# Attention and convolution block: normalisation and one addition moved to GpSimd, one copy to ScalarE, slot tables redrawn

## The chip, the cores and the metric

The program runs on one core of one Trainium2 chip. The metric is the device time of one execution in microseconds, median of several runs.

## The reference

Eight images x of 256 channels by 32x32 pixels (L = 1024 positions), all in fp32. Each image goes through two stages that matter here.

```
# stage 1: attention over the pixels, 8 heads of 32 channels
xn  = group_norm(x, 32 groups) * gn_w + gn_b
q, k, v = w_qkv @ xn + b_qkv                 # per head 32 x 1024 each
h   = w_proj @ (softmax(q'k / sqrt(32)) v) + b_proj
x   = x + h
# stage 2: tokens t = x transposed (1024 x 256)
n1  = layernorm(t)                           # norm 1
q,k = elu(n1 @ Wqk + bqk) + 1                # linear attention, rotary turn
a   = turn(q) (turn(k)^T n1 / n) * z         # z = 1 / (q . mean k + 1e-6)
t   = t + a + conv3(n1) + lepe_b             # depthwise convolution, width 3
n2  = layernorm(t)                           # norm 2
t   = t + n2 with its 2x2 Haar low band replaced by fc2(gelu(fc1(interp(low band))))
out = t transposed
```

## The kernel before

Stage 1 of image i and stage 2 of image i-1 run in one body, so there is a prologue, a first body (stage 1 of image 0 alone), six steady bodies, a last body and an epilogue (stage 2 of image 7), here called the tail. A body has 64 attention units, one for each of 2 head groups x 8 key blocks x 4 heads. In a unit, TensorE makes a 128x1024 block of scores in one of two PSUM buffers ps_s (L653), VectorE takes the negative maximum (L1053), ScalarE the exponential with its sum (L914). After every four units VectorE inverts the sums (`invert`, L1059), GpSimd scales the values with them (`scale`, L1330) and TensorE weighs the values (`values`, L668). The scores of unit s+2 wait for the exponential of unit s.

All other work is cut in steps and hung between the units by hand-written tables: one for each engine and kind of body, name -> slot numbers. Each engine runs, in each slot s, its unit instruction and then the steps due at s, in the order in which the table names them (`due`). GpSimd has no unit instruction: for it the slots give an order and nothing else. SP issues DMAs in the order of SP_ORDER. All queues are in order; semaphores join them. Results of TensorE for the steps go to two PSUM banks `work` in turn (in the tail six, four of them in ps_s); a tile may be written once the reader of the tile before it in that bank is done (READ, `claim`).

The steps that matter here, for image i-1, with the line where each works:

- proj (L727, VectorE L1153): projection, added to the residual x1, which a DMA has loaded (`residual`); x1T (L707): transposed to tokens, copied to tok by ScalarE (L965).
- stats of norm 1 (L1118, L1123), rsqrt1 on GpSimd (L1361, L1364), norm1 on VectorE (L1129): tok becomes (tok - mean) x r. lnT (L715, L977): transposed back to channels, ln_ch.
- qk (L741, ScalarE L988 and L991, VectorE L1236 `elu`), kT (L749, VectorE L1181 and L1183: turned keys), kv (L757, L1163), den and denT (L768, L774, L1189, L1191), turn on GpSimd (L507 to L514: turned queries), out (L781, VectorE L1199 into t2).
- lepe on GpSimd (L1386, L1389): the convolution, added to x1 in channels. uT (L707): that sum transposed to tokens; VectorE adds it to t2 from PSUM (L1205). Then statistics of norm 2, rsqrt2 on GpSimd, norm2 on VectorE (L1129, t2 to tok), add on GpSimd (L520, t2 + tok), pairs on GpSimd (L1395: sums of neighbours, csum).
- ll (L795, copied L996): the low band; fc1 (L800, gelu L999), fc2 (L805, L1212), rT (L715, L1003): t2 back to channels; spread: four DMAs lay the new band out for late_up (L1224), which adds it to the image; late_store writes it.
- warm: pairs of 128x128 matmuls without a use for their result (L867), in the first body and in the tail.
- For image i+1: load, group statistics (stats, moments, gn, squares, affine, apply), pq, pk, pv: queries, keys and values (L680, L692; hi L955, lo L1098).

## Time and profile before

| | us |
|---|---|
| median of 3 runs (lowest 1364.17, highest 1369.44) | 1364.28 |
| the profiled execution | 1364.11 |
| its span, first to last instruction | 1362.3 |
| TensorE / VectorE / ScalarE / GpSimd busy | 1235.3 / 995.1 / 879.5 / 467.4 |
| mean granted TensorE clock, share of full | 0.976 |

PE is TensorE's matmuls, PEld its weight loads, DVE VectorE, ACT ScalarE, POOL GpSimd, SPq SyncE's DMA queue. Lnnn is a line of the kernel. "Idle before" is the time an engine stood before an instruction, and what is behind the arrow ended that wait. Matmuls overlap, so the busy share of PE is an upper reading.

### The profile page before, as it was taken

The numbers are of one execution on the slowest core, as the hardware profiler recorded it, in microseconds if no ns is written. First come the engines' busy times: TensorE is split into PE (matmuls) and PEld (weight loads), VectorE is DVE, ScalarE is ACT, GpSimd is POOL, SyncE is SP. The second block draws the span as 40 slices with busy tenths as digits, with TensorE's granted clock in tenths as the row PEclk, the third lists the DMA queues.
The fourth block names the chain that finished last, engine by engine and source line by source line (L and its number), as shares of the span: only waits on it lengthen the run. The fifth ranks groups of instructions, "written<-read, shape, count | busy, mean of one in ns | idle before, by whom it ended". The sixth has DMA issues, their size and how long they took to land.

```text
span 1362.3 us, 22187 instructions
## 1 busy us (share of the span) xinstructions
PE 1235.3 (91%) x7972; PEld 644.5 (47%) x7972; DVE 995.1 (73%) x1609; ACT 879.5 (65%) x1457; POOL 467.4 (34%) x621
## 2 busy tenths in 40 slices
PE   6888899899998999899998999989998999979796
PEld 5544444544445454445444444454544444444373
DVE  3666687857889487866888578884879678884663
ACT  1666667675776668676775767766685767757422
POOL 2001017520285015630185203840166301850351
PEclk9998999999999999999999999999999999999897
DMA  8242415123442236223351234422262234300210
GB/s 275 58 108 45 106 40 134 34 63 101 110 112 47 52 109 139 48 63 93 92 116 27 66 117 101 105 57 58 88 140 48 62 93 110 80 15 0 80 33 31
DMA packets 51180, 110.84 MB, mean 81 GB/s; under 512 B 15456, under 2 KB 15840, under 8 KB 50816
## 3 DMA queue, kind: packets, MB, share of 16 engines
q1 hardware_dynamic: 48400, 100.39, 30.3%
q0 software_dynamic: 2480, 8.78, 2.3%
q8 instruction: 64, 1.05, 0.3%
q14 instruction: 44, 0.36, 0.1%
q10 hardware_dynamic: 192, 0.26, 0.1%
HBM read 21.81 MB, written 8.39 MB: 22 GB/s over the span
## 4 chain that ended last, share of the span: by engine, by line
PE 54%; DVE 29%; ACT 7%; issue 4%; POOL 2%; DMA 2%; SPq 1%; DVEq 0%; ACTq 0%; POOLq 0%
DVE negmax L1053 15%; PE ps_s L653 13%; PE ps_o L668 7%; PE work L741 6%; ACT probs L914 5%; PE work L680 4%; PE work L800 4%; PE work L727 4%; PE work L692 3%; DVE tok L1129 3%; DVE ln_st L1118 3%; PE work L805 3%; PE work L781 2%; DVE lo L1098 1%; PE work L715 1%
## 5 line engine op out<-in xcount | busy, mean ns | idle before, releaser
L914 ACT ACTIVATE probs<-ps_s,negmax 128x1024 f32<-128x1024 f32 x512 | 571.0, 1115 | 328.0 <-DVE negmax L1053 323.3
L1053 DVE TENSOR_REDUCE negmax<-ps_s 128x1 f32<-128x1024 f32 x512 | 618.8, 1216 | 220.0 <-PE ps_s L653 218.2
L653 PE MATMUL ps_s<-q_st,k_st 128*128 128x512 f32 x1024 | 407.8, 482 | 54.7 <-ACT probs L914 42.7
L653 PEld LDWEIGHTS ps_s<-q_st,k_st 128*128 128x128 f32 x1024 | 165.1, 192 | 294.4 <-ACT probs L914 163.3
L1330 POOL TENSOR_TENSOR v_scaled<-v_tok,rsums 128x128 f32<-128x128 f32 x128 | 56.0, 438 | 580.3 <-DVE rsums L1059 580.3
L668 PE MATMUL ps_o<-probs,v_scaled 128*32 128x512 f32 x2048 | 249.9, 606 | 1.3 <-POOL v_scaled L1330 1.3
L680 PE MATMUL work<-xg,w_qkv 128*128 128x512 f32 x256 | 120.7, 597 | 2.7 <-ACT xg L927 2.7
L741 PE MATMUL work<-ln_ch,w_qk 128*128 128x512 f32 x240 | 115.0, 601 | 3.6 <-DVE k_ch L1236 3.6
L668 PEld LDWEIGHTS ps_o<-probs,v_scaled 128*32 128x32 f32 x2048 | 53.9, 110 | 129.9 <-issue 117.7
L1389 POOL TENSOR_TENSOR x<-x,csum 128x1024 f32<-128x1024 f32 x45 | 107.5, 2389 | 2.5
L914 ACT ACTIVATION_READ_ACCUMULATOR probs<-ps_s,negmax 128x1 f32 x512 | 99.6, 195 | 0.0
L1361 POOL TENSOR_TENSOR ln_var<-ln_mv,con 128x2 f32<-128x2 f32 x64 | 12.9, 202 | 184.4 <-DVE ln_mv L1123 184.4
L800 PE MATMUL work<-band,w 128*128 128x512 f32 x120 | 63.6, 666 | 7.8 <-ACT band L996 6.0
L680 PEld LDWEIGHTS work<-xg,w_qkv 128*128 128x128 f32 x256 | 46.6, 189 | 44.2 <-issue 38.3
L692 PEld LDWEIGHTS work<-w_qkv,xg 128*128 128x128 f32 x512 | 63.6, 196 | 4.1 <-DVE lo L1098 1.4
L692 PE MATMUL work<-w_qkv,xg 128*128 128x128 f32 x512 | 64.0, 280 | 0.0
L741 PEld LDWEIGHTS work<-ln_ch,w_qk 128*128 128x128 f32 x240 | 43.0, 188 | 42.7 <-issue 29.8
L727 PE MATMUL work<-att,w_proj 128*128 128x512 f32 x120 | 56.8, 597 | 0.0
L1386 POOL TENSOR_SCALAR csum<-ln_ch,par 128x1024 f32<-128x1024 f32 x45 | 54.9, 1221 | 0.0
L805 PE MATMUL work<-shared,w 128*128 128x512 f32 x112 | 52.6, 592 | 0.0
L999 ACT ACTIVATE shared<-work,par 128x512 f32<-128x512 f32 x60 | 41.0, 689 | 16.2 <-PE work L800 16.1
L988 ACT ACTIVATE t<-work,par_elu 128x512 f32<-128x512 f32 x60 | 41.2, 687 | 10.9 <-PE work L741 10.9
(157 smaller groups left out, 1448.5 us busy)
## 6 DMA issues: line engine op xcount, KB each, us to landing
q_st<-hi SPq DMA_DIRECT2D x128, 128.0 KB, 2.4
q_st<-lo SPq DMA_DIRECT2D x120, 128.0 KB, 2.4
...
k_st<-hi SPq DMA_DIRECT2D x128, 64.0 KB, 2.8
k_st<-lo SPq DMA_DIRECT2D x128, 64.0 KB, 3.2
...
```

What stands on the lines that cost most here:

```text
L653: mm = pe.matmul(ps_s[s % 2][:, half * HALF:half * HALF + HALF], k_st[:, h, j * P:j * P + P], q_st[g][:, h, half * HALF:half * HALF + HALF ...
L668: mm = pe.matmul(ps_o[D * h:D * h + D, cols], v_scaled[:, j % 2, D * h:D * h + D], probs[:, j % 2, h, cols], start=(j == 0), stop=(j == NB ...
L680: mm = pe.matmul(bank(tile)[:, :], w_qkv[:, c, col:col + P], xg[:, c, half * HALF:half * HALF + HALF], start=(c == 0), stop=(c == NC - 1))
L692: mm = pe.matmul(bank(tile)[:, P * n:P * n + P], xg[:, c, P * nb:P * nb + P], w_qkv[:, c, col:col + P], start=(c == 0), stop=(c == NC - 1))
L727: mm = pe.matmul(ps[:, :], w_proj[:, g, P * c:P * c + P], att[:, g, half * HALF:half * HALF + HALF], start=(g == 0), stop=(g == 1))
L741: mm = pe.matmul(ps[:, :], w_qk[:, c, col:col + P], ln_ch[:, c, 1 + half * HALF:1 + half * HALF + HALF], start=(c == 0), stop=(c == NC - 1))
L800: pe.matmul(ps[:, :], w1[:, P * n:P * n + P], band[:, :], start=True, stop=True)\
L805: mm = pe.matmul(ps[:, :], w2[:, k, :], hid[:, k, :], start=(k == 0), stop=(k == 7))
L914: act.activation(probs[:, j % 2, h, :], ps_s[s % 2][:, :], ACT.Exp, bias=negmax[:, s % 4:s % 4 + 1], accum_out=sums[:, j % 2, h:h + 1]).th ...
L1053: dve.tensor_reduce(negmax[:, s % 4:s % 4 + 1], ps_s[s % 2][:, :], AX_X, ALU.max, negate=True)\
L1330: pool.tensor_tensor(v_scaled[:, j % 2, :].rearrange("p (h d) -> p h d", h=HG), v_tok[g][:, j, :].rearrange("p (h d) -> p h d", h=HG), r.t ...
L1389: pool.tensor_tensor(x1[:, c, :], x1[:, c, :], lepe_product, ALU.add).then_inc(lepe_step, 1)
```

## The change

1. Except for the last image, the layer norms (norm1, norm2) leave VectorE. GpSimd makes the shift -mean x r (two 128x1 instructions), waits for it, and writes x times r plus shift (two 128x256).
2. Except for the last image, uT is copied from PSUM to tok by ScalarE (signal u_copied, which also frees the bank), and GpSimd adds tok to t2 (`usum`).
3. proj, qk, pq, pk and values are split in two steps for TensorE, the second run right behind the first when both have the same slot; the second part of proj and qk waits for its own input only.
4. In the last image queries come before keys, and the second group's keys, turned keys and the turned queries get buffers of their own in probs, so that waits between the groups fall away.
5. All slot tables and SP_ORDER are redrawn.

```diff
 PE_STEADY = {
-    "proj": (4, 5, 7, 8), "denT": (32,), "lnT": (15, 15, 16, 17), "kv": (28, 32), "out": (35, 36, 40, 41), "ll": (48,),
-    "uT": (38, 39, 42, 42), "rT": (47, 50, 50, 51), "fc2": (52, 54, 56, 57), "pq1": (11, 12), "x1T": (9, 9, 10, 13),
+    "proj": (4, 5, 7, 8), "denT": (32,), "lnT": (15, 15, 16, 17), "kv": (28, 33), "out": (35, 36, 40, 41), "ll": (48,),
+    "uT": (37, 38, 42, 43), "rT": (47, 47, 50, 50), "fc2": (52, 55, 56, 57), "pq1": (11, 13), "x1T": (9, 9, 10, 13),
...
 ACT_STEADY = {
-    "pq0": (43, 44), "x1T": (9, 9, 11, 14), "rT": (47, 50, 50, 51), "copy": (3, 5, 34, 35),
+    "uT": (37, 38, 42, 43), "pq0": (43, 46), "x1T": (9, 10, 11, 14), "rT": (47, 47, 50, 50), "copy": (3, 5, 34, 36),
...
 DVE_STEADY = {
-    "norm1": (11, 14, 16, 16), "norm2": (42, 45, 46, 47), "uT": (39, 40, 42, 43), "late_up": (0, 5),
-    "invert": (2, 5, 8, 12, 16, 20, 25, 28, 32, 36, 41, 44, 48, 54, 56, 60), "moments": (38,), "out": (37, 37, 41, 41),
+    "uT": (38, 41, 44, 46), "late_up": (6, 13),
+    "invert": (2, 4, 8, 12, 16, 20, 25, 30, 32, 36, 41, 44, 48, 54, 57, 61), "moments": (37,), "out": (37, 37, 41, 42),
...
 POOL_STEADY = {
-    "kmean": (31,), "scale": (0, 5, 6, 12, 17, 17, 25, 27, 33, 39, 41, 45, 51, 57, 62, 63),
-    "turn": (24, 29, 31, 33, 34, 35), "rsqrt2": (39, 40, 42, 44), "add": (45, 46, 47, 50),
-    "affine": (40,), "rsqrt1": (10, 11, 13, 14), "squares": (39,), "pairs": (43, 48, 48, 50),
+    "kmean": (30,), "usum": (39, 40, 43, 43),
+    "scale": (0, 4, 6, 8, 16, 17, 25, 28, 32, 39, 41, 45, 51, 57, 61, 63), "rsqrt2": (41, 42, 43, 46),
+    "turn": (24, 28, 30, 34, 36, 38), "rsqrt1": (8, 12, 13, 14), "norm1": (12, 12, 13, 14), "squares": (40,),
+    "norm2": (41, 42, 43, 48), "pairs": (50, 50, 50, 52), "affine": (40,), "add": (43, 48, 53, 55),
...
 PE_FIRST:  "pv1" (2, 5) -> (0, 0);  DVE_FIRST: "gn" (38,) -> (40,), "moments" (38,)
...
 PE_TAIL = {
-    "proj": (0, 0, 0, 1), "x1T": (0, 0, 2, 4), "lnT": (8, 8, 14, 14), "qk": (16, 16, 16, 16, 16, 16, 16, 20),
-    "kT": (20, 20, 23, 24), "kv": (32, 33), "out": (36, 36, 36, 36), "uT": (33, 40, 40, 43), "ll": (51,),
-    "warm": (14, 15, 16 x10, 32 x8, 33, 33, 39, 43, 44 x4),
+    "proj": (0, 0, 1, 3), "x1T": (3, 3, 9, 9), "lnT": (9, 9, 12, 12), "qk": (13, 13, 15, 15, 15, 16, 16, 17),
+    "kT": (16, 17, 18, 19), "kv": (26, 28), "out": (31, 31, 34, 34), "uT": (29, 32, 35, 39), "ll": (43,),
+    "warm": (3, 3, 3, 7, 9 x4, 12 x3, 13, 17 x3, 18, 23, 24, 29, 30, 31, 31, 34, 35 x4, 36, 37 x4, 38, 39 x4, 41 x3, 54, 54),
...
 SP_ORDER = {
-    "steady": ("late_store", "late_keys0", "queries1", ..., "keys0", "residual", "spread"),
-    "last": ("late_store", "late_keys0", ..., "late_keys1", "spread", "residual"),
+    "steady": ("late_keys0", "late_store", "queries1", ..., "keys0", "spread", "residual"),
+    "last": ("late_keys0", "late_store", ..., "late_keys1", "residual", "spread"),
...
-QK_ORDER_TAIL = [(g, is_k, half) for g in range(NG) for is_k in (0, 1) for half in range(2)]
+QK_ORDER_TAIL = [(g, is_k, half) for is_k in range(2) for g in range(NG) for half in range(2)]
...
+        def q_home(b, g):
+            return q_ch[:, g, :] if b + 1 < B else probs[:, 1, g, :]
+        def k_home(b, g, half):
+            return k_ch[:, half, :] if g == 0 or b + 1 < B else probs[:, 1, 2 + half, 0:HALF]
+        def turns_home(b, g):
+            if g == 0 or b + 1 < B:
+                return rot_tok
+            return probs[:, 0, 0:2, :].rearrange("p r (b c) -> p r b c", b=NB)
...
                 elif name == "qk":
                     g, is_k, half = qk_order(b)[n]
-                    pe.wait_ge(ln_ch_done, 4 * b + 2 * half + 2)
-                    for c in range(NC):
+                    for c in parts:
+                        pe.wait_ge(ln_ch_done, 4 * b + 2 * half + c + 1)
...
+                elif name == "uT":                                   # ScalarE
+                    act.wait_ge(made["kv"], 2 * (b + 1))
+                    act.wait_ge(made[name], 4 * b + n + 1)
+                    act.copy(tok[:, 2 * n:2 * n + 2, :], ps[:, :].rearrange("p (n c) -> p n c", n=2))\
+                       .then_inc(u_copied, 1)
...
                 elif name == "uT":                                   # VectorE
-                    dve.wait_ge(attn_done, 4 * b + 2 * (n // 2) + 2)
-                    dve.wait_ge(made[name], 4 * b + n + 1)
-                    both = t2[:, 2 * n:2 * n + 2, :]
-                    dve.tensor_tensor(both, ps[:, :].rearrange("p (n c) -> p n c", n=2), both, ALU.add)\
-                       .then_inc(t2_done, 1)
-                    dve.wait_ge(t2_done, 4 * b + n + 1)
+                    if b == B - 1:
+                        ... (as before, with the signal u_copied)
+                    else:
+                        dve.wait_ge(t2_done, 4 * b + n + 1)
                     ln_statistics(b, n, t2_tokens(n), ln2_step)
...
+            def ln_scale(b, n, src, first, rsqrt, done):             # GpSimd
+                pool.wait_ge(rsqrt, 4 * b + n + 1)
+                for t in range(2):
+                    pool.tensor_scalar(ln_shift[:, n, t:t + 1], ln_mv[:, n, t, 0:1], ln_rs[:, n, t:t + 1], -1.0,
+                                       ALU.mult, ALU.mult).then_inc(first, 1)
+                pool.wait_ge(first, 8 * b + 2 * n + 2)
+                for t in range(2):
+                    nm = pool.tensor_scalar(tok[:, 2 * n + t, :], src(t), ln_rs[:, n, t:t + 1],
+                                            ln_shift[:, n, t:t + 1], ALU.mult, ALU.add)
+                nm.then_inc(done, 1)
+
+            def add_attention(b, n):
+                rows = slice(2 * n, 2 * n + 2)
+                pool.wait_ge(u_copied, 4 * b + n + 1)
+                pool.wait_ge(attn_done, 4 * b + 2 * (n // 2) + 2)
+                pool.tensor_tensor(t2[:, rows, :], t2[:, rows, :], tok[:, rows, :], ALU.add).then_inc(t2_done, 1)
```

## Rows read from the trace of the kernel before

**Rows 1.** The page: busy time, share and instructions of each engine; shares of the last chain.

```profile
PE 1235.3 (91%) x7972; PEld 644.5 (47%) x7972; DVE 995.1 (73%) x1609; ACT 879.5 (65%) x1457; POOL 467.4 (34%) x621
...
PE 54%; DVE 29%; ACT 7%; issue 4%; POOL 2%; DMA 2%; SPq 1%; DVEq 0%; ACTq 0%; POOLq 0%
```

**Rows 2.** Windows, by body: length, busy and instructions of PE, PEld, DVE, ACT, POOL, clock, DMA.

```profile
482.80:640.40 157.60, 147.23 (x959) 74.25 (x959) 121.95 (x200) 109.72 (x182) 59.77 (x77) 0.99 0.35 84
...
1113.10:1264.70 151.60, 135.11 (x894) 66.31 (x898) 113.97 (x184) 102.51 (x172) 56.97 (x67) 0.98 0.21 50
1264.70:1362.30 97.60, 77.51 (x624) 50.15 (x616) 53.56 (x113) 29.24 (x46) 33.68 (x37) 0.90 0.18 50
```

**Rows 3.** Windows, two stretches of one steady body, columns as above.

```profile
501.50:519.40 17.90, 16.14 (x84) 7.94 (x82) 17.50 (x43) 13.25 (x24) 4.31 (x10) 1.00 0.34 77
...
569.20:597.60 28.40, 24.47 (x151) 14.62 (x150) 27.68 (x58) 18.34 (x29) 14.04 (x28) 1.00 0.15 33
```

**Rows 4.** Timeline: start, length, engine, line, operation; in brackets idle before and releaser.

```profile
570.57 1.12 ACT L914 ACTIVATE probs<-ps_s,negmax 128x1024 f32<-128x1024 f32 x1 [0.39 <-DVE negmax L1053]
...
571.74 1.22 DVE L1053 TENSOR_REDUCE negmax<-ps_s 128x1 f32<-128x1024 f32 x1
...
571.83 0.73 PE L653 MATMUL ps_s<-q_st,k_st 128*128 128x512 f32 x2 [0.34 <-ACT probs L914]
...
573.05 1.12 ACT L914 ACTIVATE probs<-ps_s,negmax 128x1024 f32<-128x1024 f32 x1 [1.27 <-DVE negmax L1053]
```

**Rows 5.** Groups of instructions: count, busy us, mean ns of one, idle before them.

```profile
L1386 POOL TENSOR_SCALAR csum<-ln_ch,par 128x1024 f32<-128x1024 f32 x45 | 54.9, 1221 | 0.0
...
L1364 POOL TENSOR_TENSOR ln_rs<-ln_var,con 128x2 f32<-128x2 f32 x64 | 44.8, 700 | 5.0
...
L520 POOL TENSOR_TENSOR t<-t,tok 128x512 f32<-128x512 f32 x28 | 35.6, 1273 | 13.7 <-DVE tok L1129 13.7
...
L1129 DVE TENSOR_SCALAR tok<-t,ln_mv,ln_rs 128x256 f32<-128x256 f32 x64 | 26.4, 456 | 0.6 <-POOL ln_rs L1364 0.6
...
L1129 DVE TENSOR_SCALAR tok<-tok,ln_mv,ln_rs 128x256 f32<-128x256 f32 x64 | 22.7, 408 | 0.6 <-POOL ln_rs L1364 0.6
...
L1395 POOL TENSOR_TENSOR csum<-tok 128x256 f32<-128x256 f32 x32 | 20.1, 641 | 0.0
L1205 DVE TENSOR_TENSOR t<-work,t 128x512 f32<-128x512 f32 x28 | 19.1, 681 | 0.0
...
L965 ACT COPY tok<-work 128x512 f32<-128x512 f32 x30 | 17.0, 580 | 3.5 <-PE work L707 3.5
...
L1369 POOL TENSOR_TENSOR pool_carrier<-con 128x1 f32<-128x1 f32 x45 | 9.6, 213 | 33.2 <-ACT ln_ch L977 31.2
```

**Rows 6.** Timeline, the first matmul of the feed-forward part.

```profile
600.23 1.19 PE L800 MATMUL work<-band,w 128*128 128x512 f32 x1 [1.10 <-ACT band L996]
```

**Rows 7.** Timeline, the third transpose of normalised tokens.

```profile
519.45 0.63 PE L715 MATMUL work<-con,tok 128*128 128x128 f32 x4 [1.41 <-DVE tok L1129]
```

**Rows 8.** Timeline, VectorE and GpSimd together.

```profile
494.50 1.20 DVE L1224 SCALAR_TENSOR_TENSOR ln_ch<-csum,ln_ch 128x1024 f32<-128x1024 f32 x1
494.75 1.20 POOL L1330 TENSOR_TENSOR v_scaled<-v_tok,rsums 128x128 f32<-128x128 f32 x1 [6.73 <-DVE rsums L1059]
```

**Rows 9.** Timeline, first body, group means.

```profile
113.48 0.16 DVE L1082 COPY gn_grp<-work 128x4 f32<-128x4 f32 x1 [2.06 <-PE work L698]
```

**Rows 10.** Timeline, the tail.

```profile
1274.06 1.41 DVE L1153 SCALAR_TENSOR_TENSOR x<-work,par,x 128x512 f32<-128x512 f32 x2 [6.73 <-DMA x<-in_x]
...
1299.53 4.63 PE L867 MATMUL ps_o<-con 128*128 128x128 f32 x40
...
1313.28 0.69 DVE L1181 TENSOR_TENSOR shared<-ps_s,con 128x512 f32<-128x512 f32 x1 [2.57 <-PE work L757]
...
1321.19 0.69 DVE L1199 TENSOR_TENSOR t<-ps_s,zden 128x512 f32<-128x512 f32 x1 [0.34 <-PE ps_s L781]
...
1335.54 3.65 PE L795 MATMUL ps_s<-con,csum 128*128 128x64 f32 x16 [3.15 <-POOL csum L1395]
```

225 lines of the change are left out of this document (136 added, 89 removed), and 33 rows, old and new, of tables (ACT_LAST, ACT_STEADY, DVE_LAST, DVE_STEADY).

## The prediction

> **What bounds the kernel now.** I read the busy totals first [rows 1]: TensorE 91%, VectorE 73%, ScalarE 65%, GpSimd 34%, and a chain of work that ended last that is 54% TensorE and 29% VectorE. Then the bodies one by one, cut at the first row maximum of each [rows 2]: a steady image takes 157.6 us, in which TensorE is busy 147.2 and VectorE 122.0; the last body 151.6; what follows the last maximum, the tail, 97.6. There are six steady bodies alike. Last body against steady one: 12.1 us less TensorE work and 8.0 less VectorE work gave only 6.0 us. So neither engine alone is the bound over a whole body; they take turns.
>
> Then the stretches inside a body. The second layer norm (attention units 37 to 48 of 64, 569.2 to 597.6) lasts 28.4 us and VectorE is busy 27.7 of them, TensorE 24.5, ScalarE 18.3, GpSimd 14.0. The first (units 9 to 16) lasts 17.9 us with VectorE at 17.5, TensorE at 16.1 and GpSimd at 4.3 [rows 3]. There VectorE is the bound, and there the change acts. In the other 110 us of a body TensorE is the fuller engine.
>
> What couples the engines is the attention loop over two score banks. Its three latencies are in [rows 4]: a maximum starts at 571.74 and its exponential at 573.05 (1.31 us); the exponential of 570.57 lets TensorE start the scores after next at 571.83 (1.26 us); and these take 0.73. Everything else is hung between these by the slot tables, and every queue is in order.
>
> **The change part by part, steady body.** Removed from VectorE, per image [rows 5]: eight normalisations of the first norm at 0.41 us (3.3), eight of the second at 0.46 (3.6), four additions of the convolution at 0.68 (2.7). Together 9.6 us, of which 6.4 in the second stretch and 3.3 in the first. One of the two final 128x1024 additions (L1224, 1.20 us, [rows 8]) is moved into the first stretch (slot 5 to 13), so that stretch is relieved of 2.1 only.
>
> Added to ScalarE: four copies of 128x512 at 0.58 (2.3 us per image), in the second stretch: 18.3 becomes 20.6 of 28.4. Hidden as long as an exponential isn't behind them.
>
> Added to GpSimd: four 128x512 additions at 1.27 (5.1 us per image, the row L520 has this very form). Sixteen 128x256 scale-and-shift operations: no row has them; below is a quarter of the 128x1024 one (1221/4 = 0.31), above is the strided two-input 128x256 addition's own 0.64 in [rows 5]. I take 0.35, since the operation is the same as L1386's. Sixteen 128x1 shifts: 0.21 from the 128x1 row, about 0.18 in a pair; bounds 0.1 and 0.3. A pair of rows is normalised in 2x0.18 + 2x0.35 + a wait of 0.07 = 1.15 us (bounds 0.9 and 2.0), against 0.7 to 0.9 on VectorE. Sum: 5.1 + 8x1.15 = 14.3 us of GpSimd per image; in the second stretch 14.0 becomes 23.7 of 28.4.
>
> Ceiling of the gain: with 6.4 us off VectorE the second stretch would be bound by TensorE's 24.5, 3.9 us less; the first by TensorE's 16.1, 1.8 less. 5.7 us per image.
>
> But the chains get longer, and in-order queues wait in them. I walked the new slot order through both stretches with the latencies of [rows 4] and the prices above, from the times of this image. Second stretch: GpSimd's first addition (slot 39) stands ahead of the value scaling of the same slot and waits for ScalarE's copy at slot 37; the copy ends 572.6, the addition 574.0, the scaling 574.4, so TensorE's weighing of values comes at 574.5 instead of 572.9, and VectorE's statistics wait for the addition too. The next maxima catch up: maximum 42 starts at 581.4, as now. From slot 43 GpSimd holds one unbroken chain: two additions, rsqrt (0.21 + 0.70, 0.95 with a wait), norm 1.15, addition 1.27, scaling 0.4, rsqrt, norm, addition, three pair sums at 0.64, scaling, pair sum: 12.6 us. It starts at 585.4 (after the group norm and the first two norms) and, with two short waits for the copy of slot 43 and the statistics of slot 46, ends at 599.1. TensorE stands before it at slot 47, where the transposes rT now wait for the addition that follows the last norm (596.3; scores 49 go out 1.0 us later than now), and at ll (599.5). The first matmul of the feed-forward part starts at 600.4; now it starts at 600.23 [rows 6]. One transpose that followed it is now in front: 0.45 us back. Net -0.2 us.
>
> First stretch: rsqrt 0 stands behind a value scaling whose sums are inverted only at slot 12, so GpSimd begins at 509.1 and ends the fourth norm at 519.2. TensorE's third transpose of normalised tokens waits for it, and starts at 519.25; now it starts at 519.45 after a stall of 1.41 us on VectorE's norm [rows 7]. Net -0.2 us: one wait takes the place of the other. VectorE ends this stretch with slack that nobody uses.
>
> Contention: while VectorE ran a two-input addition in SBUF (494.50), GpSimd's scaling took 1.20 us instead of 0.40 [rows 8]. The addition now at slot 13 falls beside the norms on GpSimd: at most 1.2 us on one norm, which has 1.4 us to the next statistics. Cost 0 to 0.5.
> The Trainium skill ("SBUF — State Buffer", Who interferes with whom) says that VectorE with two SBUF inputs and a GpSimd instruction that reads SBUF block each other; the row agrees. "GPSIMD Engine Reference" (Engine selection) speaks against the change: two-input additions are to stay on VectorE, about 2x faster. What it would make of the time is the second rival below.
>
> I take -0.4 us per body, seven bodies: **-3 us** (bounds -14 and +8, from 0.9 to 2.0 per norm and 1 us of slip either way in each walk).
> Split matmul steps: each second part keeps its slot (one value step in the last body apart) and waits no longer than before: 0. SP: the residual load now stands behind the spread in steady bodies; the band is ready at about slot 58 and the residual needed at slot 5 of the next body, some ten units later: 0.
>
> **First body.** VectorE no longer waits 2.06 us for the group means [rows 9], since that step moves from slot 38 to 40; two value tiles go to unit 0. One more warm-up pair. -2 us (-4 to 0).
>
> **The tail.** The residual arrives earlier: VectorE waits 6.73 us for it now, until 1274.06 [rows 10]; in the last body its load now goes before the spread. It should bring 3.4 us, but proj 3, warm-ups and L1224 take its place before the transposes, and by my walk the fourth norm ends within 0.5 us of where it does now: 0. Then 40 warm-up instructions stand for 4.5 us ahead of the last query/key tile (1299.53), the second pair of key turns waits 2.57 us for the first kv (1313.28), and the queries are turned late. Queries first and buffers of their own (probs is free) remove these; in their place VectorE's convolution and the elus are next late: last elu 2.3 us earlier (the 4.5 us less what the convolution on VectorE then holds back), no wait (-2.6), one us of turning: first attention output at 1315.2 instead of 1321.19, -6. From there to ll the VectorE order is nearly the same (-1.2), and ll itself, which ran in 3.65 us after an idle stretch (1335.54), starts warm behind more warm-ups: -1.8. **-9 us** (bounds -14 and -2).
>
> **Sum**, on the profiled run's own 1364.1 (span 1362.3 and 1.8 around it; the median is 1364.3): 1364 - 3 - 2 - 9 = **1350 us**.
>
> **Rivals.**
> First, VectorE's relief is paid in full: my walk is too strict on GpSimd (scale-and-shift under 0.35, copies earlier). 5.7 us x 7 = 40, less 11 for tail and first body: the ceiling is 1313; half of it gives 1333. For it: VectorE is full in both stretches. Against: TensorE's transposes and ll wait on the same data by a longer way. Chance 0.17.
> Second, slower: GpSimd becomes the bound of the second norm. Place: its chain from slot 43 to ll. If a norm costs 2.0 or more there and the value scaling behind the first addition isn't made good (1.5 us), each image loses 2x0.85 + 1.5 and about 0.6 of blocking = 3.8 us: 1353 + 27 = 1380. It decides from +2.6 us per body on. For it: 23.7 of 28.4 us already. Chance 0.11.
> Third, the tail doesn't deliver (more warm-ups in TensorE's way, the turned queries late as before) and the bodies stand as they are: -4 in all, 1360. Chance 0.22.
> My own case (1341 to 1358): 0.50.
>
> **How the numbers follow.** 0.5% is 6.8 us, about what a measurement of this kernel can tell from no change. Faster: 0.48 + 0.17 + 0.02 = 0.67; same: 0.02 + 0.20 + 0.02 = 0.24; slower 0.09. The range 1332 to 1368 leaves out the upper half of the first rival and the second.
>
> **What would show it.** Steady bodies still 156 to 158 us; VectorE at about 112 us busy in each and idle before its maxima in the norm stretches; a wait of TensorE's lnT and rT transposes on GpSimd's tok and t in place of the wait on VectorE; GpSimd scale-and-shift at 0.35; tail 88 to 90 us. Wrong if bodies fall under 154 or rise over 160, or if the tail stays over 95.

## The result, and the profile after

| | before | after |
|---|---|---|
| median | 1365.54 us | 1371.13 us |
| runs | 1364.17 to 1369.44 (5) | 1369.56 to 1372.58 (5) |
| profiled run | 1364.11 us, span 1362.3 | 1371.13 us, span 1369.3 |

The ratio is 1.0038, with a 95% interval of 1.0019 to 1.0056. The forecast was 1350 us, with a range up to 1368: wrong, on the other side of no change. The page of after, its busy totals and the shares of its last chain, beside [rows 1]:

```profile
PE 1223.9 (89%) x8048; PEld 646.2 (47%) x8048; DVE 945.2 (69%) x1469; ACT 891.8 (65%) x1485; POOL 587.1 (43%) x873
...
PE 49%; POOL 20%; DVE 13%; issue 8%; ACT 7%; DMA 2%; SPq 1%; POOLq 0%; DVEq 0%; ACTq 0%
```

VectorE lost 50 us of work and 16 points of the chain; GpSimd gained 120 us and 18 points. Work that was moved took its place in the path with it.

Cut at the first maximum of each body, before and after: prologue 28.8 and 28.3; first body 139.2 and 132.6; the six steady bodies 945.0 and 954.4 (mean 157.5 and 159.1); last body 151.6 and 161.6; tail 97.7 and 92.4. The differences, -0.5 - 6.5 + 9.4 + 10.0 - 5.3, make the 7 us. First body and tail brought 12; steady bodies and last body gave 19 back. Windows of after, columns as in [rows 2]: the same steady body as there, the last body, the tail, the stretch from unit 9 to 20 of that steady body, and its second norm stretch (28.4 us in [rows 3]):

```profile
480.46:638.65 158.19, 144.06 (x959) 73.06 (x960) 114.95 (x180) 111.43 (x186) 76.82 (x113) 1.00 0.34 83
1115.60:1277.16 161.56, 139.90 (x910) 70.01 (x914) 106.98 (x165) 105.64 (x178) 74.36 (x103) 0.96 0.25 63
1277.16:1369.30 92.14, 79.45 (x680) 53.93 (x672) 53.32 (x112) 27.45 (x45) 33.60 (x37) 0.97 0.13 36
...
499.15:526.92 27.77, 23.98 (x122) 11.86 (x121) 20.57 (x39) 20.68 (x36) 12.91 (x29) 1.00 0.39 96
568.14:596.20 28.06, 22.82 (x136) 13.19 (x136) 22.60 (x47) 19.99 (x33) 21.12 (x44) 1.00 0.07 15
```

The second norm stretch (units 37 to 48 of this body) is 0.3 us shorter, as short as forecast. Units 9 to 20 are longer. The same stretch of before, one window:

```profile
501.59:527.64 26.05, 24.24 (x122) 11.99 (x121) 22.38 (x47) 20.38 (x35) 6.05 (x13) 1.00 0.47 106
```

TensorE and VectorE are less busy there than they were, ScalarE 0.3 us more, and GpSimd, with twice its old work, for less than half of it; yet the time grew by 1.7. So it is a chain, not a load. TensorE's waits in after, by releaser (total, times, longest):

```profile
PE work L772 <- POOL tok L1464: 18.4, 6, 3.1
PE ps_o L723 <- POOL v_scaled L1395: 15.8, 14, 2.1
PE work L772 <- POOL t L574: 8.7, 6, 1.5
...
PE work L856 <- POOL csum L1478: 3.8, 1, 3.8
```

L772 is the transposes of normalised tokens. Six times, once in each steady body, they wait for GpSimd's norm, 2.8 us in the first and 3.1 in the others, where they waited 1.4 for VectorE's [rows 7]. L856 is ll, and it waits 3.8 us once, in the last body. Groups of after, columns as in [rows 5]:

```profile
L1472 POOL TENSOR_TENSOR t<-t,tok 128x512 f32<-128x512 f32 x28 | 35.3, 1271 | 30.1 <-ACT tok L1039 30.1
...
L1451 POOL TENSOR_SCALAR csum<-ln_ch,par 128x1024 f32<-128x1024 f32 x45 | 53.8, 1195 | 0.0
```

The addition costs what L520 said, 1.27 us. GpSimd's two new operations, grouped by line and shape:

```profile
L1460 POOL TENSOR_SCALAR ln_shift<-ln_mv,ln_rs 128x1 f32<-128x1 f32 x112 | 31.0, 290 | 4.0
L1464 POOL TENSOR_SCALAR tok<-tok,ln_rs,ln_shift 128x256 f32<-128x256 f32 x56 | 30.4, 549 | 2.9
```

0.55 us for 128x256, not 0.35, and 0.29 for a shift, not 0.18. The same operation on four times the elements takes 1195 ns; a straight line through the two is 0.84 ns per element and 0.33 us for the instruction itself (an estimate from these two rows). My 0.35 was little more than a quarter of the large one (0.31), which prices the instruction itself at a quarter too. Two shifts (0.49), two normalisations (1.09) and a wait make 1.66 us a pair of rows, where I had 1.15.

The timeline of after in the first norm stretch, GpSimd and TensorE:

```profile
506.75 0.40 POOL L1395 TENSOR_TENSOR v_scaled<-v_tok,rsums 128x128 f32<-128x128 f32 x1 [7.18 <-DVE rsums L1133]
...
508.60 1.22 DVE L1289 SCALAR_TENSOR_TENSOR ln_ch<-csum,ln_ch 128x1024 f32<-128x1024 f32 x1
...
509.00 1.18 POOL L1460 TENSOR_SCALAR ln_shift<-ln_mv,ln_rs 128x1 f32<-128x1 f32 x2
...
515.72 0.19 POOL L1426 TENSOR_TENSOR ln_var<-ln_mv,con 128x2 f32<-128x2 f32 x1
515.99 0.70 POOL L1429 TENSOR_TENSOR ln_rs<-ln_var,con 128x2 f32<-128x2 f32 x1
...
516.80 0.49 POOL L1460 TENSOR_SCALAR ln_shift<-ln_mv,ln_rs 128x1 f32<-128x1 f32 x2
...
517.39 1.08 POOL L1464 TENSOR_SCALAR tok<-tok,ln_rs,ln_shift 128x256 f32<-128x256 f32 x2
...
518.62 0.63 PE L772 MATMUL work<-con,tok 128*128 128x128 f32 x4 [3.12 <-POOL tok L1464]
...
519.75 1.22 DVE L1127 TENSOR_REDUCE negmax<-ps_s 128x1 f32<-128x1024 f32 x1 [2.99 <-PE ps_s L707]
```

rsqrt, shift and norm of one pair take 2.75 us (515.72 to 518.47), of which I had 2.1. The fourth ends 38.2 us after the body's first maximum (at 480.22; the windows above start 0.2 us behind it); my walk had 36.5, and in before the transposes started at 36.7 [rows 7]. From the scaling at 506.75 to the end of the fourth norm GpSimd waits for nobody: 11.7 us of work in a row, and the chain of this stretch is its own. VectorE then sits idle 3 us before a maximum: its relief stands there, unused.

The fourth norm ends at this same place in the last five steady bodies (38.2 us), and 0.7 us earlier in the first, which has no 128x1024 addition beside it. What follows isn't alike. Units 17 to 20 of the six, columns as above (the third from the end is the granted clock):

```profile
196.08:208.59 12.51, 9.94 (x39) 4.74 (x40) 4.33 (x5) 8.48 (x15) 3.95 (x8) 0.86 0.60 133
355.28:369.10 13.82, 10.99 (x39) 5.71 (x40) 4.32 (x5) 8.65 (x15) 4.12 (x9) 0.75 0.53 117
515.78:526.92 11.14, 8.29 (x39) 4.08 (x40) 4.42 (x5) 8.37 (x15) 4.14 (x9) 1.00 0.66 146
673.96:686.69 12.73, 9.89 (x39) 4.92 (x40) 4.32 (x5) 8.55 (x15) 4.13 (x9) 0.87 0.57 125
833.38:844.53 11.15, 8.31 (x39) 4.09 (x40) 4.41 (x5) 8.37 (x15) 4.13 (x9) 1.00 0.65 143
991.23:1003.98 12.75, 9.91 (x39) 4.75 (x40) 4.31 (x5) 8.55 (x15) 4.13 (x9) 0.87 0.57 126
```

The same 39 matmul instructions keep TensorE busy 8.3 us in two bodies and 9.9 to 11.0 in four, where part of them ran at the lower level (1.2 GHz instead of 2.4). In front of the last five stands the same wait of 3.1 us (2.8 in the first).

### The profile page after: what moved, and what is told of

The parts are those of the page before. It is cut to its first block, busy times and chain, and to the rows that moved or that the text cites. A ratio compares the mean times of both kernels' runs of the same rounds, so it can differ in the third digit from the quotient of the medians.

```text
span 1369.3 us, 22501 instructions
## 1 busy us (share of the span) xinstructions
PE 1223.9 (89%) x8048; PEld 646.2 (47%) x8048; DVE 945.2 (69%) x1469; ACT 891.8 (65%) x1485; POOL 587.1 (43%) x873
## 4 chain that ended last, share of the span: by engine, by line
PE 49%; POOL 20%; DVE 13%; issue 8%; ACT 7%; DMA 2%; SPq 1%; POOLq 0%; DVEq 0%; ACTq 0%
PE ps_s L707 11%; PE ps_o L723 8%; DVE negmax L1127 7%; PE work L799 6%; ACT probs L982 5%; PE work L866 4%; PE work L784 4%; PE work L736 4%; POOL tok L1464 4%; PE work L861 3%; POOL ln_rs L1429 3%; POOL ln_shift L1460 2%; POOL shared L555 2%; PE work L749 2%; PE work L772 2%
## 5 line engine op out<-in xcount | busy, mean ns | idle before, releaser
L1395 POOL TENSOR_TENSOR v_scaled<-v_tok,rsums 128x128 f32<-128x128 f32 x128 | 51.2, 400 | 594.1 <-DVE rsums L1133 594.0
L799 PE MATMUL work<-ln_ch,w_qk 128*128 128x512 f32 x236 | 118.5, 627 | 3.0 <-DVE k_ch L1301 2.8
L861 PE MATMUL work<-band,w 128*128 128x512 f32 x118 | 59.2, 634 | 9.3 <-ACT band L1070 5.8
L749 PEld LDWEIGHTS work<-w_qkv,xg 128*128 128x128 f32 x512 | 63.4, 196 | 3.7 <-DVE lo L1172 0.7
L749 PE MATMUL work<-w_qkv,xg 128*128 128x128 f32 x512 | 63.6, 279 | 0.0
L866 PE MATMUL work<-shared,w 128*128 128x512 f32 x128 | 59.6, 592 | 0.0
L1451 POOL TENSOR_SCALAR csum<-ln_ch,par 128x1024 f32<-128x1024 f32 x45 | 53.8, 1195 | 0.0
L1023 ACT ACTIVATE hi<-work,par 128x512 fp32r<-128x512 f32 x48 | 32.8, 684 | 29.2 <-PE work L736 29.2
L1472 POOL TENSOR_TENSOR t<-t,tok 128x512 f32<-128x512 f32 x28 | 35.3, 1271 | 30.1 <-ACT tok L1039 30.1
```

Source lines behind the costliest of these rows:

```text
L749: mm = pe.matmul(bank(tile)[:, P * n:P * n + P], xg[:, c, P * nb:P * nb + P], w_qkv[:, c, col:col + P], start=(c == 0), stop=(c == NC - 1))
L799: mm = pe.matmul(ps[:, :], w_qk[:, c, col:col + P], ln_ch[:, c, 1 + half * HALF:1 + half * HALF + HALF], start=(c == 0), stop=(c == NC - 1))
L861: pe.matmul(ps[:, :], w1[:, P * n:P * n + P], band[:, :], start=True, stop=True)\
L866: mm = pe.matmul(ps[:, :], w2[:, k, :], hid[:, k, :], start=(k == 0), stop=(k == 7))
```

## The experiments

The time of each is given with its ratio to the kernel before on the same chip. "Steady" is the mean length of the six steady bodies in the trace (before 157.5, after 159.1). Four kernels here have before's steady tables, and their means are 156.6 to 157.8, because the granted clock falls in some of their bodies and not in others; so a difference of less than one us in this mean needs a stretch to back it. Only the tables' edits are shown.

### Where the loss sits

**First body and tail alone.** All that the change does in steady bodies and the last one is undone; the first body's tables, the split matmul steps and the tail stay.

```
 PE/ACT/DVE/POOL_STEADY, _LAST, SP_ORDER steady, last: as before
-                    if b == B - 1:   # uT: VectorE adds from PSUM
+                    if True:
```

> The changed kernel with the middle put back: the tables and SP orders of the steady bodies and of the last body are those of before, with both norms and the convolution's addition on VectorE; the first body's and the tail's tables, the split matmul steps and the tail's own buffers stay. Theory A (the two traces body by body: first body 6.5 us shorter, prologue 0.4, tail 5.3, steady bodies 9.4 longer in all, last body 10.0 longer): 1364 - 12 = 1352 us, between 1350 and 1355. Rival B (what first body and tail gain hangs on the state in which the bodies beside them leave the queues): 1358 to 1365.

1348.16 us, ratio 0.9867 [0.984, 0.9894]: 2 us below the range of A. First body 132.4, steady 156.6, last 152.5, tail 91.1. Theory A all the same: first body and tail kept their gains. The middle of the change alone costs 23 us, and without it the kernel beats both.

**The tail alone.**

```
 the kernel above, with
 PE/ACT/DVE/POOL_FIRST, SP_ORDER first: as before
```

> The kernel before in the first body, the steady ones and the last one, with only the new tail (order, buffers of its own, split matmul steps). Theory A (the first body's tables are worth 6.5 us, as its length in the trace says, and the rest of the gain of 18 us is the tail's 6 to 7 and some 5 that steady bodies vary by): 1355 (1353 to 1358). Rival B (the first body's tables only move work; the gain lies in the split matmul steps): 1347 to 1350.

1356.35 us, ratio 0.9915 [0.9887, 0.9943]; the first body is 140.0 again. Theory A: the first body's tables are worth 7 us.

**The first norm back on VectorE.**

```
 DVE_STEADY, _LAST:  + "norm1": (11, 14, 16, 16)
 POOL_STEADY, _LAST: - "norm1"
 POOL_STEADY: "scale"[3] 8 -> 12, "rsqrt1" (8, 12, 13, 14) -> (10, 11, 13, 14)
```

> The changed kernel with the first norm back on VectorE in the steady and last bodies, at the slots of before (in the steady body rsqrt1 and the fourth value scaling too); second norm, copy and addition stay moved. Theory A (GpSimd's first norm holds TensorE's transposes, 2.9 us a body): 1371 - 17 = 1354 us, 1352 to 1360, units 16 to 19 of a steady body back to about 10.7 us. Rival B (the second norm and the addition on GpSimd are what costs): 1368 to 1372.

1363.72 us, ratio 0.998 [0.9962, 0.9998]. Steady 157.5; units 9 to 20 take 27.0 us instead of 28.9 (before 26.0). Between the two: the direction is A's, the size 7 us and not 17: the last body hardly moves (161.7), and 1 us per body stays lost at units 12 to 15.

**The second norm back on VectorE.**

```
 DVE_STEADY, _LAST:  + "norm2": (42, 45, 46, 47) and (44, 45, 46, 47)
 POOL_STEADY, _LAST: - "norm2"
```

> The changed kernel with the second norm back on VectorE in the steady and last bodies, at the slots of before; first norm, copy and addition stay moved. Theory A (the second stretch of a steady body is about even between the two ways, the last body gains 3 to 7 us by it): 1364 to 1370 us. Rival B (GpSimd's second norm is the bound): 1350 to 1358. Rival C (VectorE's relief in the second stretch is worth 4 us a body): 1375 to 1390.

1377.98 us, ratio 1.009 [1.0059, 1.012]: C by its time, slower than the changed kernel, though with 2 us a body and not 4. Units 37 to 60 of steady bodies take 65.1 us instead of 63.5, at granted clocks of 0.95 to 0.97 instead of 1.00, the last body 3.8 us less. With the addition moved, the second norm on GpSimd is a help in steady bodies; in the last one it is not.

**The last body as before.**

```
 PE/ACT/DVE/POOL_LAST, SP_ORDER last: as before
-                    if b == B - 1:
+                    if b >= B - 2:
```

> The changed kernel with the last body's tables and SP order of before, its norms and addition on VectorE. Theory A (the 10 us lost in the last body come from its own order on GpSimd): 1361 us, 1359 to 1363. Rival B (they come from how the steady bodies hand over to it): 1367 to 1371.

1361.58 us, ratio 0.9961 [0.9942, 0.9979]: theory A. Last body 152.8.

### What makes the first stretch long

**A pair without shift instructions.**

```
-                for t in range(2):
-                    pool.tensor_scalar(ln_shift..., -1.0, ALU.mult, ALU.mult)
 ...
-  tensor_scalar(tok, src, ln_rs, ln_shift, ALU.mult, ALU.add)
+  tensor_scalar(tok, src, ln_mv[..., 0:1], ln_rs, ALU.subtract, ALU.mult)
```

> The changed kernel, but GpSimd normalises as (x - mean) times r, as VectorE did, so the 16 shift instructions per image fall away. Theory A (GpSimd pays a fixed cost for each instruction and then for each element, so the 128x256 instruction stays at 0.55 us and a pair falls from about 1.7 to 1.1-1.2 us): steady bodies 1 to 2 us shorter than the changed kernel's, in the stretch of units 16 to 19 above all, time 1358 to 1364. Rival B (the 128x256 instruction gets dearer with a subtraction ahead of a multiplication, or the wait is set by something else than the length of the pair): 1368 to 1373.

1428.47 us, ratio 1.0445 [1.0408, 1.0482]. B named a dearer instruction and priced it far too low (1368 to 1373): the very operation that VectorE ran in 0.41 to 0.46 us takes GpSimd 1.22 to 1.27. Its groups:

```profile
L1460 POOL TENSOR_SCALAR tok<-tok,ln_mv,ln_rs 128x256 f32<-128x256 f32 x56 | 70.5, 1269 | 1.5
L1460 POOL TENSOR_SCALAR tok<-t,ln_mv,ln_rs 128x256 f32<-128x256 f32 x56 | 67.9, 1223 | 2.6
```

A pair now takes 2.5 us instead of 1.7 and a steady body 167.7 instead of 159.1: 3.6 us more in units 9 to 20, 5.0 more in 37 to 60. So a pair's length is in the path in both stretches, and 0.85 us of it costs 8.6 us per body, more than the eight pairs' own 6.8. (Part of that is clock: 0.90 to 0.95 in units 9 to 20.)

**One product for both shifts, and a subtraction behind the multiplication.**

```
-                for t in range(2):
-                    pool.tensor_scalar(ln_shift..., -1.0, ALU.mult, ALU.mult)
+                pool.tensor_tensor(ln_shift[:, n, :], ln_mv[:, n, :, 0], ln_rs[:, n, :], ALU.mult)
 ...
-  tensor_scalar(tok, src, ln_rs, ln_shift, ALU.mult, ALU.add)
+  tensor_scalar(tok, src, ln_rs, ln_shift, ALU.mult, ALU.subtract)
```

> The changed kernel, but one 128x2 product gives both shifts (mean times r) and GpSimd computes x times r minus it. Theory A (slow is a subtraction ahead of the multiplication, and a multiplication first is fast whatever follows: 0.55 us as now; the pair loses two 128x1 instructions at 0.26 to 0.29 and gains one at 0.21, so 1.66 becomes about 1.3): steady bodies 1 to 3 us shorter, 1352 to 1364, by the slope of the run without a shift, where a pair 0.9 us longer made steady bodies 8.5 us longer. Rival B (only multiplication and addition are fast): the instruction takes 1.2 us or more, 1420 to 1440.

1439.87 us, ratio 1.0555 [1.0527, 1.0583]: rival B.

```profile
L1463 POOL TENSOR_SCALAR tok<-t,ln_rs,ln_shift 128x256 f32<-128x256 f32 x56 | 67.9, 1222 | 2.9
```

Same tiles, same order, add exchanged for subtract (the shift has its sign turned): 1222 ns against 549. The steady body is 169.2.

**The moved 128x1024 additions back at slots 0 and 5.**

```
-    "late_up": (6, 13)    (DVE_STEADY)
+    "late_up": (0, 5)
 SP_ORDER steady: "late_store" ahead of "late_keys0"
```

> The changed kernel with VectorE's two 128x1024 additions back at slots 0 and 5 of steady bodies (they stand at 6 and 13), and the late store ahead of the late keys again. Theory A (the length of GpSimd's pairs sets the stall of lnT; the contention with the VectorE addition adds 0 to 0.5 us per body): 1366 to 1371. Rival B (the contention of the addition at slot 13 with the pairs on GpSimd, one shift of which took 1.18 us, is the larger part of the stall): units 16 to 19 1.5 us shorter or more in each steady body, 1356 to 1362.

1364.65 us, ratio 0.9995 [0.9974, 1.0015], between the two. The shift that took 0.94 takes 0.26 again (both of a pair: 0.49 instead of 1.18 at 509.00 above), and the fourth norm ends 0.7 us earlier, 37.6 instead of 38.2 us into the body; in both kernels GpSimd works without a wait from that value scaling (506.75 in after) to there, so this 0.7 is the lengthened shift. Steady is 158.1, units 9 to 20 are 27.8: 1 us per body less on the mean. That mean holds clock. In the bodies at a granted clock of 1.00 units 9 to 20 take 26.05 us in before, 27.1 here, 27.8 in after. So the addition at slot 13 costs 0.7 us beside the pairs, a little over the upper end that I gave it, and the pairs 1.0.

**Matmuls that nobody needs, in the wait.**

```
 PE_STEADY: "warm": () -> (16, 16, 16, 16, 16, 16), first in the slot
```

> The changed kernel with six warm-up steps (four matmul rows each, 0.45 us) in TensorE's queue of steady bodies ahead of the third transpose of the first norm, where it waits 3.1 us for GpSimd. In the trace of the changed kernel that wait ends at the same place in all six steady bodies (38.2 us after the body's start), but units 17 to 20 then take 11.1 us in two bodies at a granted clock of 1.00 and 12.7 to 13.8 in the other four at 0.75 to 0.88. Theory A (the stall costs twice: itself, 1.7 us, and the lower clock that follows it in some bodies, 1.2 us on the mean): the clock stays at 1.00, units 9 to 20 take 27.8 us in every body instead of 28.9 on the mean, 1363 to 1367. Rival B (the clock falls for another reason, or the warm-up steps hold up the scores as much as they save): 1369 to 1375.

1365.55 us, ratio 1.0013 [0.9985, 1.004]: theory A by its time, though the interval overlaps that of after (1.0019 to 1.0056); the windows are what shows it. Units 17 to 20, the first two steady bodies:

```profile
195.32:206.22 10.90, 10.68 (x63) 6.52 (x62) 4.43 (x5) 8.51 (x15) 4.15 (x9) 1.00 0.71 156
354.83:366.02 11.19, 10.80 (x63) 6.58 (x63) 4.41 (x6) 8.51 (x15) 4.38 (x10) 1.00 0.66 146
```

GpSimd still delivers late: the fourth norm ends at the same place. But the clock stays at 1.00 in all six and units 9 to 20 take 27.7 us on the mean (27.1 to 27.8) instead of 28.9 (27.8 to 30.5). The later norm costs 1.7 us of itself (1.0 the pairs, 0.7 the addition beside them) and 1.2 on the mean through the clock behind it. A long wait just ahead is not the only way to the lower level: in a run further below (one product, in the second norm alone) TensorE waits 1.4 us here, as in before, and units 16 to 19 still take 12.2 to 12.3 us at 0.86 in five bodies, instead of 10.7 at 1.00. What lowers the clock there was not tried.

### What makes the last body long

Timeline of after, the end of its second norm:

```profile
1233.80 0.49 POOL L1460 TENSOR_SCALAR ln_shift<-ln_mv,ln_rs 128x1 f32<-128x1 f32 x2
1234.39 1.08 POOL L1464 TENSOR_SCALAR tok<-t,ln_rs,ln_shift 128x256 f32<-128x256 f32 x2
1235.56 1.26 POOL L574 TENSOR_TENSOR t<-t,tok 128x512 f32<-128x512 f32 x1
1236.78 0.61 POOL L1478 TENSOR_TENSOR csum<-tok 128x256 f32<-128x256 f32 x1
1237.45 0.98 PE L856 MATMUL work<-con,csum 128*128 128x64 f32 x4 [3.79 <-POOL csum L1478]
1239.25 3.75 PE L861 MATMUL work<-band,w 128*128 128x512 f32 x4 [0.82 <-ACT band L1070]
```

The last norm stands behind three additions and three pair sums in GpSimd's queue, ll waits 3.8 us, and then the feed-forward matmuls run at half speed: four take 3.75 us where before's took 1.96. The granted clock from 1237.4 to 1246.0 is 0.60; in before, from 1227.4 to 1236.0, it is 1.00.

This isn't all of the 10 us. Units 0 to 43 and 44 to 53 of the last body, before and after:

```profile
1113.01:1213.18 100.17, 92.24 (x703) 47.70 (x704) 84.76 (x140) 69.58 (x120) 45.88 (x50) 1.00 0.32 75
1213.18:1246.89 33.71, 27.15 (x128) 12.48 (x127) 18.27 (x34) 22.67 (x35) 10.29 (x15) 0.95 0.00 0
...
1115.37:1217.80 102.43, 95.04 (x728) 49.74 (x732) 81.61 (x130) 71.48 (x123) 54.95 (x70) 1.00 0.35 83
1217.80:1258.01 40.21, 29.60 (x116) 13.73 (x108) 13.91 (x26) 22.84 (x37) 18.62 (x32) 0.83 0.07 26
```

6.5 us lie where ll waits, 2.3 before it, and 1.2 behind it (units 54 to 62, 17.7 and 18.9 us). The changed table of this body also has four warm-up steps (slots 1, 32, 43, 60), and its two 128x1024 additions stand at slots 5 and 11 instead of 0 and 7; no run takes these out alone.

**Norms ahead of additions and pair sums.**

```
 POOL_LAST: "norm2" (43, 46, 47, 50) -> (43, 44, 46, 48), "rsqrt2"[3] 48 -> 47
 "add" (44, 46, 49, 51) -> (46, 48, 50, 52), "pairs" (46, 47, 48, 52) -> (51, 51, 51, 52)
```

> The changed kernel; in the last body alone GpSimd's order in the second norm is turned round: normalisation 1 to 3 at slots 44, 46, 48 ahead of the additions (46, 48, 50, 52) and of the pair sums (51 to 52), which stood before them (norms 46, 47, 50; additions from 44; pair sums from 46). Nothing else. Theory A (the last body is 10 us long because its norms stand behind additions and pair sums in GpSimd's queue, not because GpSimd works more): the last body 3 us shorter or more, 1364 to 1368. Rival B (it is the work and the wait for ScalarE's copies, in any order): 1370 to 1373.

1368.93 us, ratio 1.0022 [1.0, 1.0045]; last body 159.9, 1.6 us less (all of it in units 44 to 53). The time lies between the two and its interval overlaps that of after; by the last body it is closer to B: this order is a sixth of the 10 us.

**Both norms on GpSimd, the addition on VectorE.**

```
 the kernel with before's last body, with
 DVE_LAST: - "norm1", - "norm2"
 POOL_LAST: as in the changed kernel, without "usum"
```

> The changed kernel with before's last body (1361.6 us, last body 152.8), but both norms of that body on GpSimd, in the changed kernel's slots for rsqrt, norms, additions and pair sums; the convolution's addition stays on VectorE there. It parts the 9 us that the changed last body costs. Theory A (a large part is the addition on ScalarE and GpSimd, which stands ahead of the norms in GpSimd's queue): last body 154 to 156, 1363 to 1365. Rival B (the norms on GpSimd alone make it): last body 159 to 162, 1368 to 1371.

1365.0 us, ratio 0.9991 [0.9975, 1.0007]; last body 155.4: theory A. Against 152.8 the norms alone cost 2.6 us (3.1 more in units 44 to 53, the rest a little less). The other 6.2 us up to 161.6 are not the addition alone, as everything else of this body's tables changes with it: 2.5 lie in units 0 to 43, 2.0 in 44 to 53, where the addition and what waits for it stand, 1.7 in 54 to 62.

### What the second stretch is worth

**Two parts undone: first norm in steady bodies, last body.**

```
 last body as before; DVE_STEADY + "norm1", POOL_STEADY - "norm1", "scale"[3] and "rsqrt1" as with the first norm back
```

> The changed kernel with two parts undone: the first norm on VectorE in steady bodies, and the whole table set of before for the last body; the second norm and the convolution's addition stay on GpSimd and ScalarE in steady bodies. Theory A (what the two alone gave adds up: 1371 less 9.5 for the last body and 6.4, six sevenths of the 7.4, for the first norm): 1355 (1353 to 1358), so the second norm on GpSimd is still worth nothing and the version without any norm on GpSimd, 1348, stays the fastest. Rival B (the second norm and the addition on GpSimd are a gain of their own once the first norm is out of the way): under 1348.

1352.03 us, ratio 0.9888 [0.9847, 0.9928]; steady 157.6. A little under A's range and 4 us over B's: the two losses add up.

**From it, the second norm back too.**

```
 DVE_STEADY + "norm2": (42, 45, 46, 47), POOL_STEADY - "norm2"
```

> The kernel with the first norm on VectorE and before's last body (1352 us), with the second norm on VectorE too in steady bodies: what is left of the change there is the convolution's addition on ScalarE and GpSimd. Theory A (the addition moved is what costs, and the second norm on GpSimd makes it good: undoing that alone in the changed kernel cost 7 us, with 4 given back in its last body, so some 10 in six steady bodies): 1362 (1358 to 1366). Rival B (the first norm on GpSimd was what made the second dear; with it gone both forms are alike): 1349 to 1355.

1357.85 us, ratio 0.9949 [0.9934, 0.9964], just short of A's lower end: half of what A said. Units 37 to 60: 64.1 us.

**From it, one product and a subtraction.**

```
 ln_scale as in the run with one product; 24 pairs on GpSimd
```

> The kernel with the first norm on VectorE and before's last body (1352 us), and the 24 pairs left on GpSimd with one product and a subtraction. Theory A (multiplication first is fast, a pair 0.35 us shorter, one of four pairs per body in the path): 0.3 to 1 us per body, 1346 to 1350, level with the version that has no norm on GpSimd (1348). Rival B (the pair's length is hidden in the second stretch): 1351 to 1353. If the subtraction is slow: 1380 or more.

1387.14 us, ratio 1.0145 [1.01, 1.0189]: its third case, the slow subtraction (1223 ns), now in the second norm alone. Of 6.4 us per steady body 5.0 lie in units 37 to 60 (68.4 us) and 1.3 in 9 to 20, there by the lower clock named above.

**From it, the 128x1024 additions back at slots 0 and 5.**

```
 DVE_STEADY "late_up": (6, 13) -> (0, 5), SP_ORDER steady as before at its head
```

> The kernel with the first norm on VectorE and before's last body (1352 us), with VectorE's two 128x1024 additions back at slots 0 and 5 of steady bodies. Theory A (the 1.1 us that each steady body loses at units 12 to 15 against the version without any norm on GpSimd is the addition at slot 13, and the second stretch with norm and addition on GpSimd is even): 1352 less 6.6: 1345 to 1348. Rival B (the 1.1 us has another cause): 1351 to 1353.

1344.59 us, ratio 0.9834 [0.9809, 0.9859]; steady 156.3. A, and 1.2 us per body on the mean; units 12 to 15 take 8.6 instead of 9.5 in the five bodies that have the addition. So with the first norm on VectorE the addition at slot 13 costs about as much; there it stands before a norm in VectorE's own queue.

**The second norm alone on GpSimd.**

```
 first body and tail alone, with
 DVE_STEADY - "norm2"; POOL_STEADY + "norm2", with after's slots for norm2, rsqrt2, add, pairs
```

> The fastest version so far (1348 us) with the second norm alone on GpSimd in steady bodies; the convolution's addition stays on VectorE. With the runs that have both there (1352) and the addition alone (1358) it completes the square for the second stretch. Theory A (the second norm off VectorE helps wherever VectorE is full, and the addition on GpSimd is what costs; the norm gave 6 us there): 1340 to 1346. Rival B (the norm on GpSimd only makes good what the moved addition costs, and alone it lengthens the chain to the transposes): 1349 to 1356.

1344.22 us, ratio 0.983 [0.9812, 0.9849]; steady 156.3: theory A. With this the square is full. Units 37 to 60, mean of the steady bodies: both on VectorE 63.3, norm on GpSimd 62.8, norm and addition 63.4, addition alone 64.1. These means hold falls of the clock; other kernels with before's steady tables have 63.4 to 64.4 where the first corner has 63.3. In bodies at 1.00 throughout the same four are 62.8 to 63.0, 62.3 to 62.5, 63.2 to 63.6 and 63.2 to 63.4. So the norm moved alone gains 0.5 us, and the addition moved loses about 0.5 by itself and 1.0 on top of the norm. On top of the addition the norm gains nothing at the full clock; what it gains is that the clock stays there in all six bodies, where it falls in four of six with the addition alone.

Two of the corners have the change's steady tables and two those of before, and units 54 to 60 take 13.8 us with the first and 14.5 with the second, whatever is moved. So the corners are not free of the tables: in units 37 to 53 alone, those with the addition moved are 1.2 us (by itself) and 1.7 us (on top of the norm) longer, and other slots differ there as well.

### Where the first body's gain sits

**The group means' copy back at slot 38.**

```
 DVE_FIRST "gn": (40,) -> (38,), in the kernel with first body and tail alone
```

> The fastest version so far (first body and tail of the change, the rest of before, 1348 us) with VectorE's copy of the group means in the first body back at slot 38 from 40. Theory A (the wait of 2 us for it is a part of the 6.5 us that the first body gained): 1350 to 1351. Rival B (the wait is absorbed, or not the cause): 1347 to 1349.

1351.45 us, ratio 0.9884 [0.9864, 0.9903]; first body 133.3 instead of 132.4. VectorE waits 2.79 us for the copy again:

```profile
110.63 0.16 DVE L1256 COPY gn_grp<-work 128x4 f32<-128x4 f32 x1 [2.79 <-PE work L855]
```

A by its time (1351.45 against 1350 to 1351); but only 0.9 of the 3.3 us lie in the first body, and the steady bodies, whose tables are the same, are 7 us longer in this trace: the time lies at A's by luck in part. In the first body units 36 to 43 lose 2.5 us and 44 to 53 give 0.3 back; the other 1.3 lie in units 0 to 8, ahead of the copy, where it can't act. So the wait is about 2.2 to 2.5 of the 6.5 us. The rest lies at units 4 to 28 and from 44 on, where all tables differ; what makes it was not tried and stays open.

## Why the prediction was wrong, step by step

**Steady bodies: -0.4 each forecast, +1.6 measured** (units 9 to 20 +2.9; 20 to 37 and 37 to 60 -0.6 each). The step that failed is a term of the sum: 1.15 us for a pair on GpSimd, of which 0.35 for a 128x256 instruction, "since the operation is the same as L1386's". It is the same, and that row holds its price only for its own size. Measured: 1.66. My first walk had 10.1 us for GpSimd's chain in the first norm, 8.8 of work by its own prices and 1.3 of waits; there are no waits, and the work is 11.0 us without the addition beside it and 11.7 with it. So four pairs that are 0.5 us too short were in part made good by waits that didn't come: at the full clock the pairs cost 1.0 us per body, where the walk had a gain of 0.2. I had bounds of 0.9 to 2.0 for the pair, so the true value was inside, and the sum's own upper bound was +8; I chose near the low end because I took a form for a size. The second step that failed is the contention: 0 to 0.5 forecast, 0.7 measured at the full clock (the run with the additions moved back). The third is not in the sum at all: behind the longer wait of TensorE its clock falls in four of six bodies (1.2 us per body on the mean; the run with the wait filled).

**The second walk came out by its net in units 37 to 48 and not by its last mark.** Net -0.3 measured there. rT waits for the addition behind a norm (1.44 us), as said. GpSimd's chain was to run from 16.2 to 29.9 us after the maximum of unit 37, 12.6 of work and two waits; it ran from 17.3 to 30.7, 13.4 us without a wait. But the first matmul of the feed-forward part was to start 0.2 us later than before and starts 1.3 later (600.37 is 32.3 us after the maximum of unit 37, 600.23 in [rows 6] was 31.0).

```profile
585.34 2.50 POOL L1472 TENSOR_TENSOR t<-t,tok 128x512 f32<-128x512 f32 x2
...
596.25 1.06 PE L772 MATMUL work<-con,t 128*128 128x128 f32 x8 [1.44 <-POOL t L574]
...
598.13 0.61 POOL L1478 TENSOR_TENSOR csum<-tok 128x256 f32<-128x256 f32 x1
...
600.37 1.95 PE L861 MATMUL work<-band,w 128*128 128x512 f32 x4 [0.82 <-ACT band L1070]
```

That units 37 to 60 are 0.6 us shorter on the mean all the same is luck with the clock, which I hadn't forecast. Before takes 62.8 and 62.9 us at 1.00 in two bodies, and 63.8 to 65.4 at 0.95 to 0.97 in the other four; after takes 63.4 to 63.7 at 1.00 in all six. At the full clock the stretch is 0.5 us longer, not shorter. The windows of the third and fourth body of before, and of the third of after:

```profile
569.25:633.22 63.97, 58.56 (x280) 29.65 (x280) 43.18 (x74) 43.75 (x69) 15.97 (x32) 0.97 0.22 49
729.10:791.91 62.81, 57.21 (x280) 28.68 (x278) 43.08 (x74) 43.89 (x69) 15.47 (x31) 1.00 0.22 50
...
568.07:631.42 63.35, 56.54 (x280) 29.10 (x280) 38.29 (x63) 45.67 (x73) 27.00 (x52) 1.00 0.19 44
```

The -0.6 of units 20 to 37 is clock too: one body of before has 44.0 us there at 0.96, and the medians differ by 0.1. Whole bodies say the same: the shortest one, at 1.00 throughout, is 155.8 us before and 157.9 after. So the change costs a steady body 2 us at the full clock, and the measured 1.6 is that, plus 1.2 of lower clock in after, less 1.7 of it in before.

**The last body: -0.4 forecast, +10.0 measured.** The step is "seven bodies": I walked a steady body and multiplied. The last body has tables of its own: its slots put pair sums and additions ahead of the norms, ll waits for the last of them, and the clock falls behind the wait (6.5 us in units 44 to 53). The other 3.5 us are not parted further; four new warm-up steps and the 128x1024 additions at slots 5 and 11 stand there. Its rows stood in the full diff, not in the cut of it above, and I priced none.

**First body: -2 forecast, -6.5 measured.** The named wait is gone, worth 2.2 to 2.5. Fifteen value scalings, invert steps and warm-up slots were redrawn, and I costed none.

**The tail: -9 forecast, -5.3 measured.** The warm-ups ahead of the last query/key tile are gone. The last elu is 2.3 us earlier against the tail's start, as said. Then it slips. First attention output 3.0 us earlier, not 6: the step that failed is "one us of turning" and the wait's full 2.6. Between the start of the last elu and the first output 13.0 us pass (13.8 in before). The wait of 2.57 us for kv is gone, and the four turns of the keys run without a gap; but VectorE now waits 1.93 us for the output's own matmuls (0.34 in [rows 10]), and one turn of the queries runs beside GpSimd's at 3.02 us (2.71 before), so turning gave nothing. Eight warm-up matmuls (1.92 us from 1327.25) stand in TensorE's queue right ahead of the output's; how much of the 1.93 is theirs was not tried.

```profile
1317.50 0.74 DVE L1301 SCALAR_TENSOR_TENSOR probs<-ps_s,par_elu,t 128x512 f32<-128x512 f32 x1
...
1323.42 3.02 DVE L552 TENSOR_TENSOR probs<-shared,con 128x1024 f32<-128x1024 f32 x1
...
1330.52 0.69 DVE L1261 TENSOR_TENSOR t<-ps_s,zden 128x512 f32<-128x512 f32 x1 [1.93 <-PE ps_s L842]
...
1344.05 1.45 PE L856 MATMUL ps_s<-con,csum 128*128 128x64 f32 x12
```

From there to ll -0.8 (-1.2 said); ll starts at the full clock, and from it to the end -1.5 (-1.8 said). The clock of the tail is 0.97, against 0.90 in [rows 2].

**The signs that I named.** VectorE at 115 us in a steady body (112 said), the waits on tok and t present, scale-and-shift 0.55 (0.35 said), tail 92.4 (88 to 90 said). Of the bounds that I named for a wrong forecast, 160 us for a body was crossed by one in six (160.5), and 95 for the tail by none: they were set too wide to warn of 10 us in one body.

**The rivals.** The second had GpSimd as the bound from +2.6 us per body on, at 2.0 us a norm, in the second stretch. The mechanism is real, and shows most at another place: in the first stretch, where GpSimd is busy for less than half of the time. With 2.5 us a pair both stretches do what it said (+8.6 us). The third had the tail bring little, 1360: it brought 60%. The first did not happen: no steady body fell under 157 with both norms on GpSimd. The Trainium skill ("GPSIMD Engine Reference", Engine selection) has two-input operations at about half VectorE's speed and one-input ones "roughly line-rate". The first half agrees with the trace (1271 ns against 681 for the 128x512 addition, of which VectorE read one input from PSUM). The second does not for the form with a subtraction: 1269 and 1223 ns against VectorE's 408 and 456 in [rows 5]. With multiplication and addition it is 549.
